# Two batches to a matrix product in the shared expert of a two-choice mixture stage

## The reference

```python
sel = mask.T.astype(bool)
order = jnp.argsort(~sel, axis=1, stable=True)
dispatch = order[:, :capacity]                      # 320 tokens to an expert
xg = xf[dispatch]
gate = jax.nn.silu(jnp.einsum('ech,ehi->eci', xg, rg))
up = jnp.einsum('ech,ehi->eci', xg, ru)
eout = jnp.einsum('eci,eih->ech', gate * up, rd)
contrib = eout * (w * valid)[..., None]
routed = jnp.zeros_like(xf).at[dispatch.reshape(-1)].add(contrib.reshape(-1, h))
shared = jax.nn.silu(x @ sg) * (x @ su) @ sd        # inner width 1024
return shared + SCALE * routed.reshape(b, s, h)
```

## Time and profile before

| | us |
|---|---|
| median of 3 runs | 1803.29 |
| lowest, highest | 1797.32, 1804.77 |
| the profiled execution, its own time | 1801.73 |
| its span in the trace | 1799.8 |
| TensorE busy in it | 1530.6 (85%) |
| VectorE, ScalarE, GpSimd busy | 1013.2, 868.9, 632.9 |

### The profile page before, as it was taken

One profiled execution on the slowest core, in us unless ns is written; L12 is line 12 of the kernel. 1 busy time (PEld: TensorE's weight loads), 2 busy tenths in 40 slices (PEclk: granted clock), 3 DMA queues, 4 the chain that ended last, 5 costly groups with the idle time before them and its releaser, 6 DMA issues. The chain is left out here.

```text
span 1799.8 us, 31587 instructions
## 1 busy us (share of the span) xinstructions
PE 1530.6 (85%) x11327; PEld 1135.4 (63%) x11327; DVE 1013.2 (56%) x2402; ACT 868.9 (48%) x1935; POOL 632.9 (35%) x707
## 2 busy tenths in 40 slices
PE   4689978799786999996939999899996799878996
PEld 3356655566573567774827877787875577635664
DVE  6656536666275789995035554466645123535555
ACT  5455544555356677772424444544443132235552
POOL 3487603877140667772230001100013501511113
PEclk8889988899997899998859999999997899969998
DMA  7300000000000834645224000000000201300000
GB/s 218 114 13 13 13 7 2 13 13 12 13 1 9 92 65 78 77 59 113 76 71 146 1 0 1 1 1 1 1 1 7 64 15 33 37 4 2 2 2 25
DMA packets 75277, 63.71 MB, mean 35 GB/s; under 512 B 25367, under 2 KB 62790, under 8 KB 75142
## 3 DMA queue, kind: packets, MB, share of 16 engines
q1 hardware_dynamic: 65142, 53.53, 14.7%
q0 software_dynamic: 3072, 6.30, 1.7%
q10 hardware_dynamic: 6928, 2.12, 0.6%
HBM read 48.09 MB, written 9.57 MB: 32 GB/s over the span
## 5 line engine op out<-in xcount | busy, mean ns | idle before, releaser
L1355 POOL TENSOR_TENSOR inject<-delta_x,b_rows 128x512 f32<-128x512 f32 x128 | 159.5, 1270 | 82.1 <-DMA b_rows<-b_rows_dram 44.7
L1626 DVE TENSOR_TENSOR_SCAN state<-bank,inject 128x512 f32<-128x512 f32 x128 | 150.3, 1205 | 7.0 <-POOL inject L1355 4.0
L2064 POOL TENSOR_TENSOR ve<-mv,eps 128x1 f32<-128x1 f32 x32 | 6.1, 190 | 338.6 <-DVE mv L2212 338.6
L1536 ACT ACTIVATE bank<-delta,a_neg 128x255 f32<-128x255 f32 x256 | 109.0, 472 | 13.4 <-DVE state L1626 12.9
L3324 DVE TENSOR_REDUCE top<-bank 128x2 f32<-128x512 f32 (+1 forms) x96 | 61.8, 685 | 72.7 <-PE bank L3026 51.8
L2173 ACT ACTIVATE Z<-bank 128x512 f32<-128x512 f32 x64 | 34.7, 595 | 127.7 <-PE bank L2126 127.7
L2150 ACT ACTIVATE U<-bank 128x512 f32<-128x512 f32 x128 | 74.7, 593 | 41.9 <-PE bank L2087 40.8
L595 POOL TENSOR_TENSOR rotated<-rot_cos,rot_sin 128x512 f32<-128x512 f32 x56 | 70.8, 1268 | 52.0 <-DVE rot_sin L901 52.0
L1441 PEld LDWEIGHTS bank<-tabs,by_token 128*128 128x128 f32 x512 | 67.9, 196 | 24.8 <-issue 15.7
L601 POOL TENSOR_TENSOR inv_norm<-sum_sq,neghalf 128x16 f32<-128x16 f32 x28 | 82.0, 2929 | 4.2 <-POOL sum_sq L599 0.2
L638 PE MATMUL bank<-wqkv,hT 128*128 128x512 f32 x128 | 68.7, 667 | 16.4 <-ACT hT L799 13.1
(11 more groups left out here) (565 smaller groups left out, 4214.8 us busy)
## 6 DMA issues: line engine op xcount, KB each, us to landing
b_rows<-b_rows_dram SPq DMA_DIRECT2D x32, 512.0 KB, 8.9
v<-v SPq DMA_DIRECT2D x32, 130.0 KB, 2.3
slots<-zero SPq DMA_DIRECT2D x10, 256.0 KB, 3.5
rows<-slots SPq DMA_DIRECT2D x10, 256.0 KB, 4.1
moe_w<-in_L_ffn_rg_dram SPq DMA_DIRECT2D x1, 2048.0 KB, 8.7
moe_w<-in_L_ffn_ru_dram SPq DMA_DIRECT2D x1, 2048.0 KB, 13.8
wqkv<-in_L_ffn_wqkv_dram SPq DMA_DIRECT2D x2, 768.0 KB
slots_out<-y SPq DMA_DIRECT2D x8, 160.0 KB, 2.1
```

What stands on the lines that cost most here:

```text
L1355: pool.tensor_tensor(dB[:, n % R, :, :], dx[:, :, seq(n)], both(b_all[:, q % 4, n % CH, :]), ALU.mult).then_inc(s.inject.sem, 1)
L1536: last = act.activation(dA[n % RD][:, c, 1:L], delta[:, c, i * L + 1:(i + 1) * L], ACT.Exp, scale=a_neg[:, c, k:k + 1])
L1626: dve.tensor_tensor_scan(flat(h[:, n % R, :, :]), flat(dA[n % RD]), flat(dB[:, n % R, :, :]), 0.0, ALU.mult, ALU.add).then_inc(s.state.sem, 1)
```

## The change

The shared expert works on pairs of batches. Gate and up products take 512 columns, a whole bank, and so do the SiLU and VectorE's product; `sgate` and `shid` double in size. `shared_down(p)` does both batches of a pair in one go, the even one in bank 0 and the odd one in bank 7, and TensorE waits for the copy from bank 0 before it transposes the slots' rows. ScalarE copies both results of a pair after chunk 1 of the next; in the second half it copies batch 6 before the first roots and batch 7 after them. VectorE's order in the second half becomes: pair 2, combine 0 to 2, pair 3, combine 3 to 6. The columns that TensorE processes, the down products and all transfers are as they were.

```diff
@@ -2568,9 +2568,9 @@
         yg1, yg2 = sb("y_first", [P, NT, D]), sb("y_second", [P, NT, D])
         y = sb("y", [P, 2, 3, D])
         SC = IS // P
-        sgate, shid = sb("shared_gate", [P, 2, L]), sb("shared_hid", [P, 2, SC, L])
+        sgate, shid = sb("shared_gate", [P, 2, 2 * L]), sb("shared_hid", [P, 2, SC, 2 * L])
         shared = sb("shared", [P, NT, D])
-        HALF, EARLY = B // 2, B - 1
+        PAIRS, EARLY = B // 2, B - 1
         MS = [(0, P), (P, P), (2 * P, C2 - 2 * P)]
         s = open_stage(nc, net.pool, f"v:120 tables:1 mean:1 rms:1 shifted:1 exp:1 hot:1 counts:1 slots:2 rowsT_ps:5 rowsT:5 "
                        f"g_ps:{E2 * FC} u_ps:{E2 * FC} silu:{E2 * FC} hid:{E2 * FC} y_ps:{E2} y_sb:{E2} "
@@ -2587,6 +2587,7 @@
         moved, stored = net.moved2, net.stored2
         with nc.Block() as block:
             gate_bank, up_bank = (lambda c: bank[3 + c % 2]), (lambda c: bank[5 + c % 2])
+            shared_bank = lambda i: bank[7 * (i % 2)]
 
             def down(pe, e):
                 pe.wait_ge(s.hid.sem, s.hid.at(0, FC * (e + 1)))
@@ -2606,27 +2607,30 @@
                 pe.matmul(bank[2][:, 0:NT * E2], ones[:, :], flat, start=True, stop=True)
                 pe.matmul(bank[1][:, 0:NT * E2], before[:, :], flat, start=True, stop=True).then_inc(s.counts.sem, 1)
 
-                def shared_down(i):
-                    pe.wait_ge(s.s_hid.sem, s.s_hid.at(i, SC))
-                    pe.wait_ge(s.shared.sem, s.shared.at(i, 0))
-                    for t in range(TPB):
-                        tok = slice(t * P, (t + 1) * P)
-                        for c in range(SC):
-                            pe.matmul(bank[7][:, tok], shid[:, i % 2, c, tok], net.sd[:, c, :], start=(c == 0), stop=False)
-                        last = pe.matmul(bank[7][:, tok], net.xT[:, i * L + t * P:i * L + (t + 1) * P], net.tab("ident"), start=False, stop=True)
-                    last.then_inc(s.shared_ps.sem, 1)
+                def shared_down(p):
+                    pe.wait_ge(s.s_hid.sem, s.s_hid.at(p, SC))
+                    for i in (2 * p, 2 * p + 1):
+                        if i >= 2:
+                            pe.wait_ge(s.shared.sem, s.shared.at(i - 1, 0))
+                        for t in range(TPB):
+                            tok, at = slice(t * P, (t + 1) * P), i % 2 * L + t * P
+                            for c in range(SC):
+                                pe.matmul(shared_bank(i)[:, tok], shid[:, p % 2, c, at:at + P], net.sd[:, c, :], start=(c == 0), stop=False)
+                            last = pe.matmul(shared_bank(i)[:, tok], net.xT[:, i * L + t * P:i * L + (t + 1) * P], net.tab("ident"), start=False, stop=True)
+                        last.then_inc(s.shared_ps.sem, 1)
 
                 def shared_expert(first, end):
                     for i in range(first, end):
                         for c in range(SC):
                             pe.wait_ge(s.s_hid.sem, s.s_hid.at(i, max(0, c - 1)))
                             for w, to, done in ((net.sg, gate_bank(c), s.sg_ps), (net.su, up_bank(c), s.su_ps)):
-                                pe.matmul(to[:, 0:L], w[:, c * P:(c + 1) * P], net.xT[:, i * L:(i + 1) * L], start=True, stop=True).then_inc(done.sem, 1)
+                                pe.matmul(to[:, :], w[:, c * P:(c + 1) * P], net.xT[:, 2 * i * L:2 * (i + 1) * L], start=True, stop=True).then_inc(done.sem, 1)
                             if c == 1 and i > first:
                                 shared_down(i - 1)
                     shared_down(end - 1)
 
-                shared_expert(0, HALF)
+                shared_expert(0, PAIRS // 2)
+                pe.wait_ge(s.shared.sem, s.shared.at(PAIRS - 2, 1))
                 pe.wait_ge(s.slots.sem, s.slots.at(0, 2))
                 for g in range(KT // 4):
                     pe.wait_ge(parts_in[g], 16)
@@ -2646,7 +2650,7 @@
                         down(pe, e - 1)
                 down(pe, E2 - 1)
                 pe.wait_ge(s.y_sb.sem, s.y_sb.at(0, E2))
-                shared_expert(HALF, B)
+                shared_expert(PAIRS // 2, PAIRS)
                 for i in range(B):
                     pe.wait_ge(s.xn_ready.sem, s.xn_ready.at(0, i + 1))
                     if i >= 2:
@@ -2669,7 +2673,7 @@
 
                 def keep_shared(i):
                     act.wait_ge(s.shared_ps.sem, s.shared_ps.at(i, 1))
-                    act.activation(shared[:, TPB * i:TPB * (i + 1), :], bank[7][:, 0:L].rearrange("p (t d) -> p t d", d=D), ACT.Copy)\
+                    act.activation(shared[:, TPB * i:TPB * (i + 1), :], shared_bank(i)[:, 0:L].rearrange("p (t d) -> p t d", d=D), ACT.Copy)\
                         .then_inc(s.shared.sem, 1)
 
                 def shared_expert(first, end):
@@ -2677,9 +2681,10 @@
                         for c in range(SC):
                             act.wait_ge(s.sg_ps.sem, s.sg_ps.at(i, c + 1))
                             act.wait_ge(s.s_hid.sem, s.s_hid.at(i, max(0, c - 1)))
-                            act.activation(sgate[:, c % 2, :], gate_bank(c)[:, 0:L], ACT.Silu).then_inc(s.s_silu.sem, 1)
+                            act.activation(sgate[:, c % 2, :], gate_bank(c)[:, :], ACT.Silu).then_inc(s.s_silu.sem, 1)
                             if c == 1 and i > first:
-                                keep_shared(i - 1)
+                                keep_shared(2 * i - 2)
+                                keep_shared(2 * i - 1)
 
                 def deviation(k, first, end):
                     act.wait_ge(s.agg.sem, s.agg.at(0, end))
@@ -2690,8 +2695,9 @@
                     act.wait_ge(s.xnT_ready.sem, s.xnT_ready.at(0, i + 1))
                     act.activation(net.xT[:, i * L:(i + 1) * L], bank[1 + i % 2][:, 0:L], ACT.Identity).then_inc(s.x_updated.sem, 1)
 
-                shared_expert(0, HALF)
-                keep_shared(HALF - 1)
+                shared_expert(0, PAIRS // 2)
+                keep_shared(PAIRS - 2)
+                keep_shared(PAIRS - 1)
                 for g in range(KT // 4):
                     act.wait_ge(s.rowsT_ps.sem, s.rowsT_ps.at(0, g + 1))
                     act.activation(rowsT[:, g * 512:(g + 1) * 512], bank[g][:, :], ACT.Copy).then_inc(s.rowsT.sem, 1)
@@ -2705,7 +2711,8 @@
                     if e >= 1:
                         copy_y(act, e - 1)
                 copy_y(act, E2 - 1)
-                shared_expert(HALF, B)
+                shared_expert(PAIRS // 2, PAIRS)
+                keep_shared(B - 2)
                 deviation(0, 0, EARLY)
                 keep_shared(B - 1)
                 update(0)
@@ -2759,16 +2766,16 @@
 
                 weights()
 
-                def shared_batch(i):
+                def shared_pair(i):
                     for c in range(SC):
                         dve.wait_ge(s.s_silu.sem, s.s_silu.at(i, c + 1))
                         dve.wait_ge(s.su_ps.sem, s.su_ps.at(i, c + 1))
                         if i >= 2:
-                            dve.wait_ge(s.shared_ps.sem, s.shared_ps.at(i - 1, 0))
-                        dve.tensor_tensor(shid[:, i % 2, c, :], sgate[:, c % 2, :], up_bank(c)[:, 0:L], ALU.mult).then_inc(s.s_hid.sem, 1)
-
-                for i in range(HALF):
-                    shared_batch(i)
+                            dve.wait_ge(s.shared_ps.sem, s.shared_ps.at(2 * (i - 1), 0))
+                        dve.tensor_tensor(shid[:, i % 2, c, :], sgate[:, c % 2, :], up_bank(c)[:, :], ALU.mult).then_inc(s.s_hid.sem, 1)
+
+                for i in range(PAIRS // 2):
+                    shared_pair(i)
                 for e in range(E2):
                     for c in range(FC):
                         j = FC * e + c
@@ -2805,17 +2812,12 @@
                         last = dve.tensor_scalar(yg2[:, t, :], yg1[:, t, :], mv[:, t, 0:1], rstd[:, t:t + 1], ALU.subtract, ALU.mult)
                     last.then_inc(s.xn_ready.sem, 1)
 
-                shared_batch(HALF)
-                combine(0)
-                shared_batch(HALF + 1)
-                combine(1)
-                combine(2)
-                shared_batch(HALF + 2)
-                combine(3)
-                combine(4)
-                shared_batch(HALF + 3)
-                combine(5)
-                combine(6)
+                shared_pair(PAIRS // 2)
+                for i in range(3):
+                    combine(i)
+                shared_pair(PAIRS // 2 + 1)
+                for i in range(3, EARLY):
+                    combine(i)
                 inverse(0, 0, EARLY)
                 for i in range(4):
                     normalise(i)
```

## The result

| | before | after |
|---|---|---|
| median, us (runs) | 1801.18 (5) | 1788.93 (5) |
| lowest, highest | 1797.24, 1804.77 | 1788.65, 1793.05 |
| profiled execution, its own time | 1801.73 | 1793.05 |
| its span | 1799.8 | 1791.2 |

The ratio is 0.9942, with a 95% interval of 0.9922 to 0.9963: the changed kernel is 0.4 to 0.8% faster, 10.4 us by the ratio, 12.2 by the medians, 8.6 by the two spans. Forecast were 7.8 us and 1795.5; the median lies near the lower edge of the range. The ratio says more than 0.5%, to which I gave 0.38, but its interval reaches from 0.4%.

The account below looks back on a forecast made before the run. TensorE bounds the first half, gathers the second. Start, cover, L of 7.9 us, one 6.7 us stop and 10 us of lower clock put transposes at 1446.3 against 1454.11: gain 7.8, 1795.5 us; range 1793 to 1799, 8-in-10 1788.5 to 1804.

Parts of the forecast that it names:

- the single stop: First half, behind the double down block: TensorE waits 6.7 us, against stops of 2.33 and 6.02 before.
- nothing from the second half: Second half: TensorE's part ends some 2 us sooner, into the wait for gathers, so gain 0.
- Start: First half's beginning: TensorE begins the third wide step at 1392.4 with four old steps done; gain 1.4 us.
- the lower clock after the stop: First half, after the stop: 10 us of lower clock, three wide steps at 3.45 us and one at 1.73.
- L: Lateness of TensorE's down results beside indirect transfers: 7.9 us after the double block, the sum of 2.1 and 5.8.
- rival 2: First half: slowness is a rate, not a delay; only the start's gain stays, 1.6 us with boundary stops, 1801.7; chance 0.13.
- The 22 us of work in 40: First half, 1397.5 to 1435: the rate at which TensorE gets through work however it is cut.
- Rival 1: First half: lateness doesn't grow with the block or is covered; slots' rows then bind; gain 14, 1789 us; chance 0.22.
- The rule of the Trainium skill: DMA and compute engines can't slow one another, except where GpSimd's descriptor writing meets a VectorE lock.
- Rival 3: First half: double block's result unseen until scatters are over; 3.4 us slower, 1806.7; decides from L = 15.7; chance 0.07.
- Rival 4: Second half: gathers make results late too; last combine waits for the copy, 6.6 us lost, 1802; chance 0.08.
- its banks alternate, so the copy of the first batch is hidden: Double down block, 8.04 us in one piece: the first batch's copy is hidden under the second batch.

Follow-up runs that it names:

- first_half_pairs: Changed kernel with pairs only in the first half, batches by themselves in the second with VectorE's old order; 1788.79 us, ratio 0.994 to the kernel before.
- second_half_pairs: Changed kernel with batches by themselves in the first half, pairs only in the second; 1797.08 us, ratio 0.9995 to the kernel before.
- before_again: The kernel before, unchanged, measured again; 1798.99 us against 1798.10 for the same kernel, ratio 1.0018.
- downs_last_b: Changed kernel with both first-half down blocks after all its gate and up steps, on a chip with lateness; 1792.51 us, ratio 0.9937 to the kernel before.
- narrow_steps: Changed kernel with first-half gate and up products cut into four of 128 columns, each with its own load; 1805.78 us, kernel before 1803.16 (one run each).
- turned_downs_b: Changed kernel with down weights stationary and 256 hidden columns moving, half the down records, on a chip with lateness; 1792.51 us (one run), kernel before 1804.75.
- the first four experiments: Four variants of the changed kernel on one chip: down blocks last, double block cut in two, scatters after the half, down products turned; kernel before 1783.89 us there.
- downs_last: Changed kernel with both first-half down blocks after all its gate and up steps; 1787.28 us, ratio 1.0019 to the kernel before.
- two_blocks: Changed kernel with the double down block cut in two, behind chunks 1 and 3 of the next pair; 1789.05 us, ratio 1.003 to the kernel before.

## Why the prediction was right, and where it was off

**The first half, by its steps.** Right: the place of the gain, the single stop (6.7 forecast, 6.87), its end (39.8 us after the first product forecast, 40.7 measured), a lower clock behind it, and nothing from the second half, which first_half_pairs (0.994) and second_half_pairs (0.9995) show apart. Start: the third wide step at 1391.85, 6.9 us after the first product, forecast 6.8. Up to the end of the double block 30.2 us, forecast 29.7.

**The term that was off** is the lower clock after the stop. I took 10 us of it, as before, which gave 1446.3 for the transposes. The granted clock was 0.50 from 1429 to 1430 and 1.00 from then on; it had fallen at 1423, while TensorE still stood, so that less than two of the wide steps ran at the lower level where I had three. From the end of the stop to the transposes it took 18.28 us instead of 20.9. These 2.6 us are more than the difference of the two gains in this half, 9.6 against 7.8; the rest went the other way, in the 0.9 us by which the stop ended later than forecast.

**The profiled execution of before was a good one.** From its first shared product to its first routed one it takes 71.75 us. The same first half takes 75.91 in before_again and 73.82 in second_half_pairs. (Some 28 us of it lie at the lower clock in before_again, 15 in the profiled execution.) The changed first half takes 62.19, 62.29 and 62.24 in its three traces with lateness. So the gain lies between 9.6 and 13.7 us, and the medians' 12.2 is inside it. A sum against one trace could not have it.

**L was right for a reason that I had wrong.** I took the lateness as a delay that goes with a block, added 2.1 and 5.8, and noted rival 2, a rate, as the other reading. Of the down products rival 2 was right; its time, 1801.7, was not, since the wide steps hardly share in it. (The 22 us of work in 40 that I gave for it are those from 1398.24 to 1438.22 and not from 1397.5 to 1435.) Records of 128 columns take 0.26 us (changed kernel, 9.34 us between two copies), 0.28 (downs_last_b) and 0.27 (narrow_steps) beside the scatters instead of 0.112. Before, the 36 records of the batch from 1416.51 gave their result after 9.98 us, 0.28 each. The rate isn't a constant: the first batch's 36 records take 0.17 before, 0.20 after and 0.22 in downs_last_b. Both kernels run the down products of two batches, 72 records, beside the scatters, and pay about the same for them: 16.6 us after, 16.3 before, 16.4 in before_again, but 18.1 in second_half_pairs. So that the sum of two came out to 0.2 us is in part luck.

It also says why the pairs gain. The slow pace looks the same for a wider record: before, behind its first stop, steps of four 256-column records start 1.44 and 1.45 us apart, the four to 1.43 us of downs_last_b, instead of 0.86:

```profile
1409.76 0.70 PE L2624 MATMUL bank<-xT,sg 128*128 128x256 f32 x2 [0.32 <-issue]
...
1411.21 0.70 PE L2624 MATMUL bank<-xT,sg 128*128 128x256 f32 x2 [0.32 <-DVE shared_hid L2768]
```

That is 0.36 us a record, above the 0.216 that 256 columns take at full pace and below the 0.43 of 512. So a wide step, 1.72 us, has room for it. This step is worked out from the rates and not tried by itself, and three things blur it. The first batch's steps of before keep their 0.86 beside the scatters until 1397. In turned_downs_b the records of 256 columns kept their pace in one block and were 2 us late in the other. And there two wide steps, from the SiLU at 1422.36 to that at 1426.47, took 1.95 and 2.16 us, so 512 columns don't always escape.

**Rival 1** asked what happens with no lateness: bound by the rows, 1789. The changed kernel's median is 1788.93, but its trace shows the lateness at full size, so this is chance. Yet the rival is true elsewhere. On the chip of the first four experiments nothing is late, transposes wait 3.8 to 5.2 us for rows, and the kernel before runs in 1783.9. There pairs aren't faster: downs_last 1.0019, two_blocks 1.003. The changed kernel itself was not run there, nor the trace of before taken. Where rows are next in line the pairs may even cost something: from GpSimd's first scatter to SyncE's request for the rows it is 47.2 us after and 45.2 before, by a pause in the scatters (see the open questions). The rule of the Trainium skill that I set against the trace (page "SBUF — State Buffer", section "SBUF: two separate sides") fits that chip. In the first measurement and on the three other chips, where the kernel before takes 1798 us or more, the traces show TensorE slowed beside GpSimd's indirect transfers, and there they decide.

**Rival 3** fell: L was 8.05, far from 15.7. **Rival 4** fell in its price: the last copy is late, by 4.3 us, but the longest stop among TensorE's shared products there is 1.03 us, and the copy starts at 1559.01, before the last combine's rows are in.

**My step "its banks alternate, so the copy of the first batch is hidden"** held, and TensorE's wait for bank 0 costs nothing: its copy starts at 1440.10, the transposes at 1443.91.

**Open.** Why one chip doesn't show the slow records; each chip was used on one occasion, so chip and occasion aren't told apart. What in an indirect transfer slows TensorE: direct ones of the same bytes don't (one run), but GpSimd's work for each and the pattern of rows differ together. When the slow pace sets in, since before, the first steps beside scatters kept theirs. And the first pause between runs of scatters is 3.50 us after and 1.53 before. It is 2.96 to 3.74 in every run with wide steps beside indirect scatters, 1.54 in narrow_steps and second_half_pairs, but 2.52 in before_again, so the width of the steps doesn't settle it; no run looked further.

## What to carry to other kernels

Where GpSimd's indirect transfers run beside TensorE, count the matmul records and not only the columns: fewer and wider products can gain there though the columns stay the same, and a rewrite in narrow ones can lose (the first half of narrow_steps took 77.5 us instead of 62.2). Read when a result is used, not when the record says that it ended. Before a gain that rests on such a loss is believed, look at the kernel on a second chip: here it was 0.6% in two sets of runs, and on one chip its variants gained nothing: no result was late there, and the transposes waited for the rows.

## What was unexpected in the hardware

- Beside indirect scatters an fp32 record of 128 columns with its own load takes 0.26 to 0.28 us instead of 0.112 once the slow pace has set in, on three of the four chips of the experiments. At the slowest it is four records to 1.43 us, for 128 columns (downs_last_b) and for 256 (before).
- TensorE's recorded starts run ahead of its work. In downs_last_b, when 36 down records are done (copy at 1424.94), 66 have a start; at the next result (72 done, 1435.08) it is 103: 30 and 31 records ahead, and each has its own load. The Trainium skill, page "TensorE: Matmul & The Clock Gate", section "Architectural detail: the array is 16× 32×32, not 1× 128×128", gives the engine a queue of 64; 30 or 31 products with as many loads are 60 to 62, and the trace agrees.
- The kernel before took 1784 us on one chip and 1798 to 1805 on the three others.
